# Forward stage: places of the group two back ahead of the normalisation, its gates behind it, both ahead of the second gate product

## The chip, the core and the metric

The kernel runs on one core of a Trainium2 chip. Its engines are TensorE (PE in the rows, its weight loads PEld), VectorE (DVE), ScalarE (ACT), GpSimd (POOL) and SyncE (SP, which only issues transfers here). Each has its own stream of instructions and waits for the others by semaphores. The metric is the time of one execution on the device in microseconds (us); lower is better.

## The reference, cut to what matters

Two layers of attention-like and feed-forward blocks over 8 x 512 tokens of 128 features. The change lies where the third block ends (its adapted weights `theta` applied to the queries) and the fourth, a mixture of eight experts, chooses its rows.

```python
    h_q = jax.nn.swish(q_ttt @ theta['gate']) * (q_ttt @ theta['val'])
    o = h_q @ theta['proj'] @ proj_w + proj_b
...
    logits = xt @ Wg + bg
    probs = jax.nn.softmax(logits, axis=-1)
    gate_vals, exp_idx = jax.lax.top_k(probs, K)          # K = 2 of E = 8
    gate_vals = gate_vals / jnp.sum(gate_vals, axis=-1, keepdims=True)
    capacity = int(np.ceil(CF * T * K / E))
    eidx = exp_idx.T.reshape(-1)
    oh = jax.nn.one_hot(eidx, E, dtype=jnp.int32)
    pos = jnp.sum((jnp.cumsum(oh, axis=0) - oh) * oh, axis=-1)
    keep = pos < capacity
    buf = buf.at[eidx, pos_c].add(jnp.where(keep[:, None], xk, 0.0))
```

`xt` is the layer-normalised sum of the input and `o`. So for each token the kernel needs its normalisation, its two experts, the two gates, and its place in each expert's list, which is a count over the tokens before it.

## The kernel before, in words

The forward stage works in eight groups (`g`) of 512 tokens, four tiles of 128. The hidden width of 512 is worked in four chunks (`c`), numbered through as `z = 4g + c`. What each engine does in a group, in its written order (nothing is scheduled by a program; the order in the code is the order on the engine):

- TensorE: for each chunk two products of 128 x 512 (gate and value, into a ring of three pairs of banks); behind chunk 0, from g = 2, `earlier_choices(g - 2)`, the small counting matmuls (64, then up to 48 columns) whose sum is `pos`; they wait for the choices of that group and for the router sums of group g - 1. Behind chunk 3 comes `fwd_out(g)`, the output product: 16 matmuls (32 rows of the trace) of 136 columns into four quarters of two banks. It waits for all four gate products of VectorE. A product of TensorE for chunk c = 3 waits for the gate product of chunk 0 of its group, one of the next group's chunk 0 for that of chunk 1.
- ScalarE: silu of each chunk (L1446); ahead of chunk 2 `scaled_tokens(g - 1)` (L1432, four instructions), which waits for the normalisation.
- VectorE: `moments(g - 1)` (L2296 the residual add, which waits for the output product, L2299 the router sums, mean and variance up to L2314); then the gate products of the four chunks (L2421, here called products 0 to 3), each of which waits for its silu; behind product 0 `normalise_tokens(g - 1)` (L2320 to L2330), which waits for GpSimd's power; behind product 1, from g = 2, `gates_of(g - 2)` (L2376 to L2380) and `places(g - 2)` (L2390 to L2402); behind product 3 `choices(g - 1)` (L2342 to L2369).
- GpSimd: a power L1130 (the root of the variance of group g - 1 and the exponential of group g - 2 in one instruction), which waits for the moments; then the last two scatters of the group before (L1116, indirect transfers that write rows of tokens to the experts' lists in HBM), and then six scatters of group g - 2, which wait for that group's gates, scaled tokens and places.

Behind the eight groups two more rounds (g = 8 and 9) finish the choices, in the order places, normalisation, gates at g = 8. When all 64 scatters have landed, the experts' rows are loaded.

The steps inside normalisation, gates and places each wait for the one ahead on the same engine. All three parts write tiles that the others don't read.

Of the kernel before, what the change touches and what calls it, by code (L numbers as in the profile page):

```python
# [33 lines left out]
def build(nc, L0_attn_x, L0_attn_W_pe, L0_attn_b_pe, L0_attn_stt_energy, L0_attn_W_fc, L0_attn_gamma,  # L34
# [18 lines left out]
    with ExitStack() as ctx:  # L53
# [115 lines left out]
        CHUNKS = [(24, 7), (18, 6), (12, 6)]  # L169
        NCH = len(CHUNKS)  # L170
        CH_END = [sum(n for _, n in CHUNKS[:c + 1]) for c in range(NCH)]
        v_taps = [(k, c) for c, (lo, n) in enumerate(CHUNKS) for k in range(lo + n - 1, lo - 1, -1)]
        assert len(v_taps) == NDVE and NPOOL % PT == 0
# [1794 lines left out]
        def _(dve):  # L1968
# [87 lines left out]
            for b in range(NB):  # L2056
                more, i = b + 1 < NB, 0
                for what in DVE_ORDER:
                    kind, g = what.rstrip("0123"), int(what[-1]) if what[-1] in "0123" else 0
# [231 lines left out]
            def moments(g):  # L2291

                base = RS * g
                dve.wait_ge(f_o.sem, f_o.at(g + 1))
                tiles = slice(g * TPB, (g + 1) * TPB)
                TT(X[:, tiles, :], quarter[:, :, 0:D], X[:, tiles, :], ALU.add).then_inc(x3_ready.sem, x3_ready.unit)  # L2296
                if g == 0:
                    dve.wait_ge(rt["lx"].sem, rt["lx"].at(3))
                TT(GL, quarter[:, :, D:D + NE], router_x[:, tiles, :], ALU.add).then_inc(rt["raw"].sem, rt["raw"].unit)  # L2299
                dve.wait_ge(x3_ready.sem, x3_ready.at(g + 1))  # L2300
                for j in range(TPB):
                    ins = v.bn_stats(g_stats[:, j, :], X[:, g * TPB + j, :])
                ins.then_inc(rs.sem, rs.unit)
                dve.wait_ge(rs.sem, rs.at(base + 1))
                mean_e, m2_e, mean_o, m2_o = (g_stats[:, :, f] for f in (1, 2, 4, 5))
                TT(gs[:, 0, :], mean_e, mean_o, ALU.add)
                TT(gs[:, 1, :], mean_e, mean_o, ALU.subtract)
                TT(gs[:, 2, :], m2_e, m2_o, ALU.add).then_inc(rs.sem, rs.unit)
                dve.wait_ge(rs.sem, rs.at(base + 2))
                v.tensor_scalar(gs[:, 8, :], gs[:, 0, :], 0.5, None, ALU.mult)  # L2310
                v.tensor_scalar(gs[:, 5, :], gs[:, 2, :], 1.0 / D, LN_EPS, ALU.mult, ALU.add)
                v.scalar_tensor_tensor(gs[:, 6, :], gs[:, 1, :], 0.25, gs[:, 1, :], ALU.mult, ALU.mult).then_inc(rs.sem, rs.unit)
                dve.wait_ge(rs.sem, rs.at(base + 3))
                TT(powers[:, 0, 0:TPB], gs[:, 5, :], gs[:, 6, :], ALU.add).then_inc(rt["ve"].sem, rt["ve"].unit)  # L2314

            def normalise_tokens(g):

                base = RS * g
                dve.wait_ge(rt["inv"].sem, rt["inv"].at(g + 1))
                TT(gs[:, 5, :], powers[:, 2, 0:TPB], powers[:, 2, 0:TPB], ALU.mult).then_inc(rs.sem, rs.unit)  # L2320
                dve.wait_ge(rs.sem, rs.at(base + 4))
                TT(gs[:, 6, :], gs[:, 5, :], powers[:, 0, 0:TPB], ALU.mult).then_inc(rs.sem, rs.unit)
                dve.wait_ge(rs.sem, rs.at(base + 5))
                v.tensor_scalar(gs[:, 5, :], gs[:, 6, :], -0.5, 1.5, ALU.mult, ALU.add).then_inc(rs.sem, rs.unit)
                dve.wait_ge(rs.sem, rs.at(base + 6))
                if g:
                    dve.wait_ge(rt["xn"].sem, rt["xn"].at(g))
                TT(gs[:, 7, :], gs[:, 5, :], powers[:, 2, 0:TPB], ALU.mult).then_inc(rs.sem, rs.unit)
                dve.wait_ge(rs.sem, rs.at(base + 7))
                v.scalar_tensor_tensor(gs[:, 12, :], gs[:, 8, :], -1.0, gs[:, 7, :], ALU.mult, ALU.mult).then_inc(rt["scale"].sem, rt["scale"].unit)  # L2330
# [40 lines left out]
            def gates_of(g):  # L2371

                tiles, gt = slice(g * TPB, (g + 1) * TPB), rt["gated"]
                ratio, first, apart = powers[:, 2, TPB:], XR[:, tiles, D + 1], XR[:, tiles, D + 2]
                dve.wait_ge(rt["inv"].sem, rt["inv"].at(g + 2))
                v.tensor_scalar(gg, ratio, 1.0, None, ALU.add).then_inc(gt.sem, gt.unit)  # L2376
                dve.wait_ge(gt.sem, gt.at(3 * g + 1))
                v.reciprocal(first, gg).then_inc(gt.sem, gt.unit)
                dve.wait_ge(gt.sem, gt.at(3 * g + 2))
                v.scalar_tensor_tensor(apart, ratio, -1.0, first, ALU.add, ALU.mult).then_inc(gt.sem, gt.unit)  # L2380

            def places(g):

                tiles, ps, base = slice(g * TPB, (g + 1) * TPB), rt["place"], PS * g
                oh = OHK[:, tiles, :]
                dve.wait_ge(rt["prefix_mm"].sem, rt["prefix_mm"].at(g + 1))
                dve.wait_ge(rt["index"].sem, rt["index"].at(g + 1))
                at = D + NE
                pos = quarter[:, 3, at:at + TPB * NEK].rearrange("p (c e) -> p c e", e=NEK)
                v.tensor_scalar(gk[:, 0], pos, float(CAP), 1e6, ALU.is_ge, ALU.mult)  # L2390
                TT(gk[:, 1], pos, place_sign[:].unsqueeze(1).to_broadcast([P, TPB, NEK]), ALU.mult).then_inc(ps.sem, ps.unit)
                dve.wait_ge(ps.sem, ps.at(base + 1))
                TT(gk[:, 2], gk[:, 1], place_base[:].unsqueeze(1).to_broadcast([P, TPB, NEK]), ALU.add)
                TT(run[:], run[:], gr, ALU.add).then_inc(ps.sem, ps.unit)
                dve.wait_ge(ps.sem, ps.at(base + 2))
                TT(gk[:, 1], gk[:, 0], gk[:, 2], ALU.add).then_inc(ps.sem, ps.unit)
                dve.wait_ge(ps.sem, ps.at(base + 3))
                TT(gk[:, 3], gk[:, 1], oh, ALU.mult).then_inc(ps.sem, ps.unit)
                dve.wait_ge(ps.sem, ps.at(base + 4))
                v.tensor_reduce(gp.rearrange("p c k -> p (c k)"), gk[:, 3].rearrange("p c (k e) -> p (c k) e", e=NE), AX.X, ALU.add).then_inc(ps.sem, ps.unit)  # L2400
                dve.wait_ge(ps.sem, ps.at(base + 5))
                v.tensor_copy(put_at[:, g * TPB * TOPK:(g + 1) * TPB * TOPK], gp.rearrange("p c k -> p (c k)")).then_inc(rt["put"].sem, rt["put"].unit)  # L2402
                dve.wait_ge(rt["put"].sem, rt["put"].at(g + 1))

            dve.wait_ge(rt_made.sem, rt_made.at(10))
            for g in range(NB + 2):
                if 1 <= g <= NB:
                    moments(g - 1)
                if g < NB:
                    s = g % 2  # L2410
                    for c in range(HC):
                        z = g * HC + c
                        if c == 1 and g:
                            normalise_tokens(g - 1)
                        if c == 2 and g >= 2:
                            gates_of(g - 2)
                            places(g - 2)
                        dve.wait_ge(f_sr.sem, f_sr.at(z + 1))
                        if c == 0:
                            dve.wait_ge(f_o.sem, f_o.at(g + 1 - 2))  # L2420
                        TT(f_h[:, s, c, :], f_s[:, z % FRING, :], bank[2 * (z % FRING) + 1][:], ALU.mult).then_inc(f_hr.sem, f_hr.unit)  # L2421
                elif g == NB:
                    places(g - 2)
                    normalise_tokens(g - 1)
                    gates_of(g - 2)
                else:
                    places(g - 2)
                    gates_of(g - 2)
                if 1 <= g <= NB:
                    choices(g - 1)  # L2430
# [110 lines left out]
```

## Time and profile before

| | us |
|---|---|
| median of three runs | 1357.92 (1357.22 to 1360.12) |
| the profiled execution, its own time | 1356.87 |
| its span in the profile | 1354.8 |
| busy: TensorE / VectorE / GpSimd / ScalarE | 1131.4 / 902.9 / 542.5 / 489.7 |
| forward stage, first gate product to the last output product's add | 1008.2 to 1121.9 |
| tail of scatters behind it, last one starts | 1149.3 |

The shares are means over stages with different limits, so the prediction reads the forward stage alone. In a row of the timeline stand: start, duration, engine, line, operation, what it writes and reads, how many instructions are merged, and in brackets the idle time of the engine ahead of it and what ended that.

### The profile page before, as it was taken

How to read it: one execution, taken by the hardware profiler on the slowest of the kernel's cores; microseconds unless marked ns; L12 is line 12 of the kernel's file. 1: busy time of each engine (PE TensorE's matmuls, PEld its weight loads, DVE VectorE, ACT ScalarE, POOL GpSimd, SP SyncE). 2: the span in 40 equal slices, each digit the busy share in tenths (PEclk: the TensorE clock that was granted, in tenths of full speed). 3: DMA queues.
4: the chain of work that ended last, by engine and by line, in shares of the span. 5: the costliest groups of instructions: out<-in, count | busy, mean ns of one | idle time of the engine just before them, and what ended most of it. 6: DMA issues, size and time to landing. Idle time of an engine off the chain costs nothing.

```text
span 1354.8 us, 15992 instructions
## 1 busy us (share of the span) xinstructions
PE 1131.4 (84%) x4801; PEld 682.0 (50%) x4801; DVE 902.9 (67%) x2031; ACT 489.7 (36%) x957; POOL 542.5 (40%) x453
## 2 busy tenths in 40 slices
PE   3899999964867668999999899999989872798981
PEld 1444444432456454555556555555555541575761
DVE  5788888888889686777777577777746673423220
ACT  3544444445435563222223222222232220455441
POOL 4788788984346234000000000000003557176776
PEclk9899999986989988999999999999999896898996
DMA  4422222200000041000080000000000122556432
GB/s 138 123 60 60 61 60 60 60 0 1 0 1 0 6 158 63 16 23 15 23 324 20 1 24 15 23 15 16 17 8 28 52 87 94 138 115 132 75 42 22
DMA packets 66191, 73.86 MB, mean 55 GB/s; under 512 B 10223, under 2 KB 44369, under 8 KB 65617
## 3 DMA queue, kind: packets, MB, share of 16 engines
q1 hardware_dynamic: 52369, 64.46, 15.3%
q0 software_dynamic: 13504, 8.62, 4.4%
q8 instruction: 29, 0.48, 0.1%
q14 instruction: 33, 0.27, 0.1%
q10 hardware_dynamic: 256, 0.03, 0.0%
HBM read 29.73 MB, written 28.02 MB: 43 GB/s over the span
## 4 chain that ended last, share of the span: by engine, by line
PE 36%; POOL 9%; issue 9%; DVE 4%; DMA 2%; ACT 1%; POOLq 1%; SPq 0%; DVEq 0%; ACTq 0%
PE banks L1708 33%; POOL out_dram L1154 6%; POOL expert_in_scratch L1116 2%; PE banks L1743 2%; DMA out_dram<-arena 2%; POOL powers L1130 1%; PE banks L1763 1%; DVE arena L2421 0%; DMA arena<-expert_in_scratch 0%; ACT arena L1401 0%; DVE arena L2273 0%; DVE arena L2277 0%; DVE arena L2281 0%; DMA expert_in_scratch<-arena,put_at 0%; POOLq L53 0%
## 5 line engine op out<-in xcount | busy, mean ns | idle before, releaser
L1708 PE MATMUL banks<-arena 128*128 128x128 f32 (+4 forms) x1480 | 381.9, 396 | 16.3 <-ACT arena L1467 7.2
L1708 PEld LDWEIGHTS banks<-arena 128*128 128x128 f32 (+1 forms) x1480 | 204.3, 190 | 88.0 <-issue 57.5
L1580 PE MATMUL banks<-arena,ident 128*128 128x512 f32 x368 | 172.4, 600 | 10.8 <-DVE arena L2038 9.6
L1154 POOL DMA_INDIRECT out_dram<-arena x80 | 127.7, 1596 | 71.6 <-issue 35.6
L1022 POOL TENSOR_TENSOR arena<-arena 128x512 f32<-128x512 f32 x96 | 112.3, 1196 | 14.3 <-ACT arena L1195 14.3
L1580 PEld LDWEIGHTS banks<-arena,ident 128*128 128x128 f32 x368 | 67.0, 191 | 87.4 <-issue 64.0
L1112 POOL IOTA arena<- 128x32 f32 x1 | 0.2, 215 | 262.7 <-DVE ttt_val_w L2284 262.7
L1388 ACT ACTIVATE arena<-banks 128x512 f32<-128x512 f32 x64 | 38.2, 597 | 175.1 <-PE banks L1743 175.1
L2038 DVE TENSOR_TENSOR arena<-arena,banks 128x512 f32<-128x512 f32 x152 | 96.1, 674 | 0.5 <-PE banks L1580 0.5
L1708 PEld LDWEIGHTS banks<-ttt_proj_w,arena 128*128 128x128 f32 x512 | 67.8, 194 | 31.7 <-issue 29.2
L1029 POOL TENSOR_TENSOR arena<-arena 128x512 f32<-128x512 f32 x64 | 81.3, 1270 | 5.0
L1110 POOL TENSOR_TENSOR router_x<-router_x,router_b 128x256 f32<-128x256 f32 x1 | 0.7, 727 | 204.3 <-ACT router_b L1409 204.3
L2223 DVE TENSOR_TENSOR arena<-arena,banks 128x512 f32<-128x512 f32 x64 | 44.0, 687 | 51.3 <-PE banks L1708 51.1
L1116 POOL DMA_INDIRECT expert_in_scratch<-arena,put_at x64 | 62.9, 982 | 33.5 <-issue 21.8
L1708 PE MATMUL banks<-ttt_proj_w,arena 128*128 128x128 f32 x512 | 68.6, 278 | 0.0
L1708 PE MATMUL banks<-ttt_gate_w,arena 128*128 128x512 f32 x128 | 67.2, 607 | 0.7 <-issue 0.7
L1708 PE MATMUL banks<-ttt_proj_wT,arena 128*128 128x512 f32 x128 | 65.6, 594 | 0.7 <-ACT arena L1393 0.7
L1708 PE MATMUL banks<-ttt_val_w,arena 128*128 128x512 f32 x128 | 66.0, 598 | 0.0
L1382 ACT ACTIVATE arena<-banks 128x512 f32<-128x512 f32 x64 | 38.2, 598 | 69.6 <-PE banks L1708 68.4
L2209 DVE TENSOR_TENSOR arena<-banks,arena 128x512 f32<-128x512 f32 x64 | 44.2, 691 | 15.2 <-PE banks L1708 15.2
L1467 ACT ACTIVATE arena<-banks,b_s 128x410 f32<-128x410 f32 (+1 forms) x84 | 49.2, 600 | 10.1 <-PE banks L1708 5.0
L1454 ACT ACTIVATE arena<-arena 128x128 f32<-128x128 f32 x80 | 26.0, 391 | 72.4 <-DVE arena L2478 62.1
(351 smaller groups left out, 2123.0 us busy)
## 6 DMA issues: line engine op xcount, KB each, us to landing
arena<-arena SPq DMA_DIRECT2D x64, 224.0 KB
arena<-expert_in_scratch SPq DMA_DIRECT2D x14, 589.5 KB
expert_in_scratch<-arena SPq DMA_DIRECT2D x4, 1244.5 KB
expert_in_scratch<-arena SPq DMA_DIRECT2D x5, 982.5 KB
arena<-kT_scratch SPq DMA_DIRECT2D x16, 256.0 KB, 2.6
arena<-k_scratch SPq DMA_DIRECT2D x16, 256.0 KB, 2.6
arena<-in_L_ffn_W_dram SPq DMA_DIRECT2D x16, 256.0 KB
kT_scratch<-arena SPq DMA_DIRECT2D x8, 256.0 KB
```

Source lines behind the costliest of these rows:

```text
L1022: pool.tensor_tensor(out=by_heads(dst), in0=window(b, k), in1=ws[:, b % 2, :, k:k + 1].to_broadcast([P, HT, HD]), op=ALU.mult).then_inc(po ...
L1029: ins = pool.tensor_tensor(out=unit, in0=unit, in1=ptmp[:, i, :], op=ALU.add)
L1116: pool.indirect_dma_start(out=buf_dram, out_offset=bass.IndirectOffsetOnAxis(ap=put_at[:, a:a + 1], axis=0), in_=XR[:, a // TOPK, :], in_o ...
L1154: pool.indirect_dma_start(out=out_rows_dram, out_offset=bass.IndirectOffsetOnAxis(ap=y_at[0:r, s, j:j + 1], axis=0), in_=yo[0:r, q, j % 4, ...
L1382: nc.scalar.activation(t_sig[:, q, :], bank[0][:], ACT.Sigmoid).then_inc(tt["sig"].sem, tt["sig"].unit)
L1388: nc.scalar.activation(hT[:, q, :], bank[2][:], ACT.Copy).then_inc(tt["hT"].sem, tt["hT"].unit)
L1467: nc.scalar.activation(hE[:, c, at:at + w], bank[2 + q][:, 0:w], ACT.Gelu_apprx_tanh, bias=b1_s[:, s, c:c + 1]).then_inc(ex["gelu"].sem, e ...
L1580: m = nc.tensor.matmul(bank[ACC[b % 2]][:], ident[:], src, start=first, stop=last)
L1708: return nc.tensor.matmul(out_, lhsT, rhs, start=start, stop=stop)
L2038: nc.vector.tensor_tensor(by_heads(prodv[:, n % NV, :]), window(b, k), bank[WB[q % 2]][:, (k - lo) * HT:(k - lo + 1) * HT].unsqueeze(2).to ...
L2209: TT(t_da[:, q, :], bank[4][:], t_m[:, q, :], ALU.mult).then_inc(tt["da"].sem, tt["da"].unit)
L2223: TT(t_h[:, q, :], t_s[:, q, :], bank[1][:], ALU.mult).then_inc(tt["h"].sem, tt["h"].unit)
```

## The change

In groups 2 to 7, VectorE does the places of the group two back directly behind product 0, ahead of the normalisation, and that group's gates directly behind the normalisation, ahead of product 1. Before, both stood between products 1 and 2. Products 1, 2 and 3 then follow one another. The rounds g = 0, 1, 8 and 9 and all other engines keep their order. A line is added, so the gate product's line is L2422 in the changed kernel.

```diff
@@ -2410,11 +2410,12 @@
                     s = g % 2
                     for c in range(HC):
                         z = g * HC + c
+                        if c == 1 and g >= 2:
+                            places(g - 2)
                         if c == 1 and g:
                             normalise_tokens(g - 1)
-                        if c == 2 and g >= 2:
+                        if c == 1 and g >= 2:
                             gates_of(g - 2)
-                            places(g - 2)
                         dve.wait_ge(f_sr.sem, f_sr.at(z + 1))
```

VectorE in group 2 before, from the last instruction of the moments to the start of places; semaphores are shared by names, so ln_std stands for the power and wqT_mm for the counting matmuls:

```order
L2314 TENSOR_TENSOR powers<-arena 128x4 [waits fp4_step]
L2421 TENSOR_TENSOR arena<-arena,banks 128x512 [waits f_o,f_s]
L2320 TENSOR_TENSOR arena<-powers 128x4 [waits ln_std]
L2322 TENSOR_TENSOR arena<-arena,powers 128x4 [waits fp4_step]
L2324 TENSOR_SCALAR arena<-arena 128x4 [waits fp4_step]
L2328 TENSOR_TENSOR arena<-arena,powers 128x4 [waits ln_out,fp4_step]
L2330 SCALAR_TENSOR_TENSOR arena<-arena 128x4 [waits fp4_step]
L2421 TENSOR_TENSOR arena<-arena,banks 128x512 [waits f_s]
L2376 TENSOR_SCALAR arena<-powers 128x4 [waits ln_std]
L2378 RECIPROCAL arena<-arena 128x4 [waits e_exp]
L2380 SCALAR_TENSOR_TENSOR arena<-powers,arena 128x4 [waits e_exp]
L2390 TENSOR_SCALAR arena<-banks 128x64 [waits wq_ready,wqT_mm]
```

The same engine from the same place in the changed kernel, up to the instruction that waits for the power:

```order
L2314 TENSOR_TENSOR powers<-arena 128x4 [waits fp4_step]
L2422 TENSOR_TENSOR arena<-arena,banks 128x512 [waits f_o,f_s]
L2390 TENSOR_SCALAR arena<-banks 128x64 [waits wq_ready,wqT_mm]
L2391 TENSOR_TENSOR arena<-banks,place_sign 128x64
L2393 TENSOR_TENSOR arena<-arena,place_base 128x64 [waits nrm_step]
L2394 TENSOR_TENSOR run<-run,arena 128x16
L2396 TENSOR_TENSOR arena<-arena 128x64 [waits nrm_step]
L2398 TENSOR_TENSOR arena<-arena 128x64 [waits nrm_step]
L2400 TENSOR_REDUCE arena<-arena 128x8 [waits nrm_step]
L2402 CAST put_at<-arena 128x8 [waits nrm_step]
L2320 TENSOR_TENSOR arena<-powers 128x4 [waits ln_std,q_scaled]
```

So the wait for the counting matmuls has moved ahead of the wait for the power. Further on in the same group of the changed kernel, from the end of the normalisation to the start of the choices:

```order
L2330 SCALAR_TENSOR_TENSOR arena<-arena 128x4 [waits fp4_step]
L2376 TENSOR_SCALAR arena<-powers 128x4 [waits ln_std]
L2378 RECIPROCAL arena<-arena 128x4 [waits e_exp]
L2380 SCALAR_TENSOR_TENSOR arena<-powers,arena 128x4 [waits e_exp]
L2422 TENSOR_TENSOR arena<-arena,banks 128x512 [waits f_s] x3
L2342 TENSOR_TENSOR arena<-arena 128x32 [waits unit_ready,xqT_mm]
```

Before, product 1 stood ahead of L2376, and places stood between L2380 and the other two products.

## Rows read from the trace of the kernel before

**Rows 1.** Waits of DVE, 1005 to 1180 us: waiter, releaser, us, times, longest

```profile
DVE X L2296 <- PE banks L1708: 14.2, 6, 4.1
```

**Rows 2.** Timeline of one group on DVE: residual add to products 2 and 3

```profile
1060.24 0.69 DVE L2296 TENSOR_TENSOR X<-banks,X 128x512 f32<-128x512 f32 x1 [3.53 <-PE banks L1708]
...
1062.64 0.69 DVE L2421 TENSOR_TENSOR arena<-arena,banks 128x512 f32<-128x512 f32 x1
...
1064.51 0.16 DVE L2320 TENSOR_TENSOR arena<-powers 128x4 f32<-128x4 f32 x1 [1.19 <-POOL powers L1130]
...
1064.90 0.17 DVE L2324 TENSOR_SCALAR arena<-arena 128x4 f32<-128x4 f32 x1
...
1065.38 0.68 DVE L2421 TENSOR_TENSOR arena<-arena,banks 128x512 f32<-128x512 f32 x1
...
1065.98 0.23 DVE L2376 TENSOR_SCALAR arena<-powers 128x4 f32<-128x4 f32 x1
...
1066.54 0.22 DVE L2390 TENSOR_SCALAR arena<-banks 128x64 f32<-128x64 f32 x1
...
1068.25 1.28 DVE L2421 TENSOR_TENSOR arena<-arena,banks 128x512 f32<-128x512 f32 x2
```

**Rows 3.** Timeline of the same group on PE and ACT

```profile
1061.60 0.79 PE L1708 MATMUL banks<-arena,ident 128*128 128x48 f32 x6
...
1065.50 1.65 ACT L1432 ACTIVATE arena<-X,arena 128x128 f32<-128x128 f32 x4 [0.66 <-DVE arena L2330]
...
1067.05 1.22 ACT L1446 ACTIVATE arena<-banks 128x512 f32<-128x512 f32 x2
...
1069.59 3.98 PE L1708 MATMUL banks<-PW,arena 128*128 128x136 f32 x32 [1.95 <-DVE arena L2421]
```

**Rows 4.** Timeline of the same group on POOL: power, second late scatter, first of six

```profile
1062.81 1.67 POOL L1130 TENSOR_TENSOR powers<-powers 128x8 f32<-128x8 f32 x1 [2.38 <-DVE powers L2314]
...
1066.01 0.97 POOL L1116 DMA_INDIRECT expert_in_scratch<-arena,put_at  x1 [0.30 <-issue]
...
1069.10 0.97 POOL L1116 DMA_INDIRECT expert_in_scratch<-arena,put_at  x1 [2.12 <-DVE put_at L2402]
```

**Rows 5.** Timeline: output products and the adds behind them, three groups

```profile
1026.22 3.97 PE L1708 MATMUL banks<-PW,arena 128*128 128x136 f32 x32 [1.41 <-DVE arena L2421]
...
1030.23 0.69 DVE L2296 TENSOR_TENSOR X<-banks,X 128x512 f32<-128x512 f32 x1 [0.91 <-PE banks L1708]
...
1076.27 0.69 DVE L2296 TENSOR_TENSOR X<-banks,X 128x512 f32<-128x512 f32 x1 [3.52 <-remote]
...
1116.66 3.97 PE L1708 MATMUL banks<-PW,arena 128*128 128x136 f32 x32 [1.95 <-DVE arena L2421]
...
1121.92 0.69 DVE L2296 TENSOR_TENSOR X<-banks,X 128x512 f32<-128x512 f32 x1 [2.10 <-PE banks L1708]
```

**Rows 6.** Timeline of the end of the stage, rounds g = 8 and 9

```profile
1123.28 0.79 PE L1708 MATMUL banks<-arena,ident 128*128 128x48 f32 x6
...
1124.49 1.67 POOL L1130 TENSOR_TENSOR powers<-powers 128x8 f32<-128x8 f32 x1 [0.94 <-issue]
...
1124.89 0.23 DVE L2390 TENSOR_SCALAR arena<-banks 128x64 f32<-128x64 f32 x1 [0.49 <-PE banks L1708]
...
1125.28 0.22 DVE L2393 TENSOR_TENSOR arena<-arena,place_base 128x64 f32<-128x64 f32 x1
...
1126.60 0.16 DVE L2320 TENSOR_TENSOR arena<-powers 128x4 f32<-128x4 f32 x1
...
1126.99 0.37 DVE L2324 TENSOR_SCALAR arena<-arena 128x4 f32<-128x4 f32 x1
...
1149.29 0.97 POOL L1116 DMA_INDIRECT expert_in_scratch<-arena,put_at  x1 [0.30 <-issue]
```

**Rows 7.** Windows (busy of PE, PEld, DVE, ACT, POOL, then PEclk) and timeline: a slower output product

```profile
1055.50:1057.50 2.00, 2.00 (x11) 2.00 (x10) 1.08 (x6) 0.00 (x0) 1.57 (x2) 0.52 0.20 67
...
1053.56 5.64 PE L1708 MATMUL banks<-PW,arena 128*128 128x136 f32 x32 [1.99 <-DVE arena L2421]
```

## The prediction

> **What bounds the kernel now.** I read the views in this order: the waits of VectorE over the forward stage, one group on all engines in order of time, and last the end of the stage. No engine is at its limit there: TensorE, ScalarE, VectorE and GpSimd hand each group on to each other. The largest wait of VectorE within the stage is the one of the residual add L2296 for the output product, 14.2 in six waits [rows 1]. I look at the group that begins when that add starts at 1060.24 [rows 2] and ends when it starts again at 1076.27 [rows 5]: 16.03 us.
>
> In it one cycle runs: add at 1060.24, moments, product 0 at 1062.64 [rows 2]; GpSimd's power from 1062.81, 1.67 long [rows 4]; VectorE idles 1.19 and starts the normalisation at 1064.51 [rows 2]; product 1 at 1065.38, gates at 1065.98, places at 1066.54, products 2 and 3 from 1068.25, ending 1069.53 [rows 2]; the output product of TensorE at 1069.59 [rows 3]; the next add at 1076.27 [rows 5]. So 9.35 us belong to the add-to-output-product part and 6.68 to the output product until VectorE sees it.
>
> The second part is longer than the matmuls. Without scatters running, the output product started at 1026.22 and the add followed at 1030.23, 4.01 later. Here it is 6.68, and in the last group 1121.92 - 1116.66 = 5.26 [rows 5]. The excess, 1.25 to 2.67 in these two, is there only in groups in which GpSimd scatters. GpSimd itself isn't the bound before the last group: it idles before each run of six scatters (2.12) [rows 4] and before the power. After the last moments it is: from 1124.49 it works without a pause worth naming to the last scatter at 1149.29 [rows 6], and the experts' first load waits for that. What the change brings must therefore bring 1124.49 forward.
>
> **The change part by part.** No instruction is added or removed. In groups 2 to 7 the eight instructions of places go ahead of the normalisation, into the idle time behind product 0; the three of gates go ahead of product 1.
>
> Places, 1068.25 - 1066.54 = 1.71 [rows 2]. Now it can start one product pitch (1065.98 - 1065.38 = 0.60) behind product 0: 1063.24. Its input, the counting matmuls, begin their last part at 1061.60 and take 0.79 [rows 3], so it doesn't wait. It ends at 1064.95. The power is ready for VectorE at 1064.51: of the 1.71, 1.27 lie in idle time and 0.44 delay the normalisation. The cover is thus the 1.19 of idle time [rows 2] and some wake-up time; without it places would cost its whole 1.71.
>
> Normalisation, 1065.38 - 1064.51 = 0.87, from 1064.95: ends 1065.82. Gates, 0.56, to 1066.38. Products 1, 2 and 3 at a pitch of 0.60 could then start at 1066.38, 1066.98 and 1067.58 on VectorE, against 1068.85 for product 3 before. This 1.27 is not what comes out, for ScalarE is next: it scales the tokens when the normalisation is ready (1065.50, that is 0.99 after its start), runs the third activation 1.55 later at 1067.05, and two activations take 1.22 [rows 3]. With the normalisation 0.44 later: 1065.94, 1067.49, 1068.71. Product 3 follows at 1068.74, takes 0.68, and the output product starts at about 1069.48 instead of 1069.59. **Gain 0.11.**
>
> One thing takes this back. At the end of the stage (g = 8, already ordered places, normalisation) the tensor_scalar L2324 took 0.37 [rows 6], where it takes 0.17 in the group [rows 2]. It started 0.83 behind the end of the power (1126.99 against 1126.16), with a scatter under way. In the changed groups it starts at 1064.95 + 0.39 = 1065.34, 0.86 behind the end of the power, at the same phase of the same scatter. I count 0.20 more: output product at 1069.68, **0.09 later than before**. Both ends stay: -0.11 and +0.09; I take the second, as the row is nearest in kind.
>
> This holds for the four groups in which TensorE idles about 1.95 before the output product, as in [rows 3, 7]. In the timeline of TensorE the other two idle 1.41, as the group without places does [rows 5]: there the last activation already sets product 3, and 0.44 to 0.64 of delay fit into its slack: nothing. Sum: 4 x 0.09 = +0.4, bounds -0.4 and +0.4.
>
> The scatters move too. Places' result comes at 1064.95 instead of 1068.25, gates' at 1066.38 to 1066.58. GpSimd is still in its two late scatters: the second starts at 1066.01, lasts 0.97 [rows 4], so 1066.98, and about 0.44 behind it the run of six begins: 1067.42 instead of 1069.10, **1.7 earlier**. At a pitch of 1.28 its last scatter then begins at 1073.8 and ends at 1074.8, before 1076.5. By itself that gains nothing, as GpSimd waits for the next moments anyway, and after the last moments the tail of scatters is as long as before. It changes only what lies beside the output product.
>
> Product 1 comes up to 1.2 us later. Nobody misses it: of its readers the earliest is the next group's first pair of matmuls, behind the output product. The earlier end of places frees the output product's bank earlier, and that wait isn't the last one either.
>
> **Clock.** One output product ran at the granted clock 0.52, that is the 1.2 GHz level, after TensorE had idled 1.99, and took 5.64 instead of 3.97 [rows 7]. The idle times before and after stay within 0.2 of what they were, so I count no change, but 1.7 us per such product for the range.
>
> **The rivals.** *A, the likeliest:* only the order's sum. The profiled run took 1356.87 (its span 1354.8 and 2.1 around it); with +0.4 it is 1357.3. The median of the runs is 1.05 above the profiled one, so 1358.3. With the bounds of the sum and one output product at the other clock level more or less: 1356.0 to 1360.4.
>
> *B, the output product's end is seen earlier.* For it: the delay beyond 4.01 exists only in groups with scatters, and the six now end sooner. Before, the add started 0.8 behind the start of the sixth scatter (1069.10 + 5 x 1.28 = 1075.5, and 1076.27) [rows 4, 5]. If that bounds it, the add now comes by 1073.8 + 0.8 = 1074.6, a gain of 1.6 in this group. The last group, whose delay is 1.25, would gain about 0.4 by the same rule, and the four between some 2 in all: 4 us, hence 1354.3; if the delay went altogether, 1351. Against it: the six scatters still cover the whole output product, and under the same six scatters one group shows an excess of 2.67 and the last 1.25. This trace doesn't show what makes it.
>
> *C, slower: places waits for the counting matmuls.* Places now stands ahead of everything that ScalarE and the output product wait for. At the end of the stage the counting matmuls ended at 1123.28 + 0.79 = 1124.07, and places, with VectorE idle, started only at 1124.89, 2.97 behind the add [rows 6]. In a changed group its turn comes 3.00 behind the add (1063.24 - 1060.24): a slack of 0.03. Each us that the matmuls are seen later is then a us for the group. With 0.6 in each of six groups: 1358.3 + 3.6 = 1361.9. It decides from 0.5 per group. Against it: the matmuls ended 0.9 before that turn in this group, and the late arrival at the end of the stage still lies before this point.
>
> *D, GpSimd's power and places hold each other out.* Places now runs under the power, and L2393, L2396 and L2398 read two operands in SBUF. If they waited for its end, L2393 would move from 1063.63 to 1064.5: 0.9 more in up to six groups, 1363. The end of the stage speaks against it: the power ran from 1124.49 to 1126.16, L2393 started at 1125.28, and places took 1126.60 - 1124.89 = 1.71 [rows 6], as long as without a power beside it.
> By the Trainium skill ("SBUF — State Buffer", Who interferes with whom) such an instruction and a GpSimd instruction that reads SBUF exclude each other for the whole instruction, which is the time of D; the trace doesn't agree for these small shapes.
>
> That the change does not do what it says is excluded for the order itself, but not for its purpose: if product 3 is set by ScalarE, nearly nothing of the freed time arrives. That is A.
>
> **How the numbers follow.** A 0.53, B 0.27, C 0.16, D 0.04. A difference of 0.2%, 2.7 us, is about what measurement can tell from none. B lies beyond it on one side, C and D on the other, A within; so faster 0.27, same 0.53, slower 0.20. The range 1353.4 to 1361.5 takes in A whole and reaches into B and C until 2 in 10 are out.
>
> **What would show it.** Right: in a changed group the idle time before the normalisation is gone, places takes 1.71 about 0.6 behind product 0, the run of six scatters starts about 4.8 behind product 0 instead of 6.5, and the output product about 7.0 behind it as before. L2324 at 0.37 shows the loss, at 0.17 the gain. B would show as less than the 5.3 to 6.7 between the output product and the add; C as idle time before L2390, released by TensorE; D as a stretched L2393. Wrong would be a product 3 that is not released by ScalarE, or a different count of output products at the lower clock.

## The result and the profile after

| | before | changed |
|---|---|---|
| median of 20 runs each, us | 1357.78 (1355.07 to 1361.22) | 1362.15 (1358.02 to 1364.06) |
| profiled execution, its own time / its span | 1356.87 / 1354.8 | 1362.42 / 1360.4 |
| first residual add of the stage / last one | 1017.98 / 1121.92 | 1019.27 / 1127.32 |
| between these two | 103.94 | 108.05 |
| last add to the end of the last scatter | 28.34 | 28.17 |

The ratio of the runs is 1.0023, with a 95% interval of 1.0013 to 1.0032. So the changed kernel is slower by 3.1 us (0.0023 x 1357.8; by the interval 1.8 to 4.3), which gives 1360.9 where 1358.3 was predicted. The medians are 4.4 apart. In the two profiles the stage is 4.1 longer. Another 1.3 lies ahead of the first changed instruction and isn't the change's. Each profile shows one execution, and the 20 times of either kernel spread over 6 us: the two profiled times are 5.6 apart, the runs 3.1 to 4.4. So the group-by-group figures below belong to these two executions.

First the group that begins at 1047.24, on VectorE, as [rows 2] of before (start, duration, engine, line, operation; in brackets the idle time ahead and its releaser):

```profile
1047.24 0.69 DVE L2296 TENSOR_TENSOR X<-banks,X 128x512 f32<-128x512 f32 x1 [3.26 <-remote]
...
1049.64 0.69 DVE L2422 TENSOR_TENSOR arena<-arena,banks 128x512 f32<-128x512 f32 x1
1050.24 0.22 DVE L2390 TENSOR_SCALAR arena<-banks 128x64 f32<-128x64 f32 x1
...
1050.62 0.23 DVE L2393 TENSOR_TENSOR arena<-arena,place_base 128x64 f32<-128x64 f32 x1
...
1051.95 0.16 DVE L2320 TENSOR_TENSOR arena<-powers 128x4 f32<-128x4 f32 x1
...
1052.34 0.35 DVE L2324 TENSOR_SCALAR arena<-arena 128x4 f32<-128x4 f32 x1
...
1053.55 0.68 DVE L2422 TENSOR_TENSOR arena<-arena,banks 128x512 f32<-128x512 f32 x1
1055.28 1.28 DVE L2422 TENSOR_TENSOR arena<-arena,banks 128x512 f32<-128x512 f32 x2 [1.05 <-ACT arena L1446]
...
1063.26 0.69 DVE L2296 TENSOR_TENSOR X<-banks,X 128x512 f32<-128x512 f32 x1 [3.53 <-remote]
```

The order does what it was worked out to do. Places begin 0.60 behind product 0 (1050.24) and take 1.71 to 1051.95; there is no idle time ahead of L2390 nor of L2320; L2324 takes 0.35. Product 2 starts when ScalarE has released it. Product 3 then follows on VectorE at the pitch of 0.60: the two activations of ScalarE are over at 1055.73 (below, 1054.68 + 1.05), ahead of its start at 1055.89. The same group on TensorE:

```profile
1056.62 3.97 PE L1708 MATMUL banks<-PW,arena 128*128 128x136 f32 x32 [1.99 <-DVE arena L2422]
1060.43 1.02 PE L1708 MATMUL banks<-arena,ttt_gate_w 128*128 128x512 f32 x2
1061.29 1.02 PE L1708 MATMUL banks<-arena,ttt_val_w 128*128 128x512 f32 x2
...
1073.75 3.97 PE L1708 MATMUL banks<-PW,arena 128*128 128x136 f32 x32 [1.41 <-DVE arena L2422]
```

and on ScalarE:

```profile
1053.12 1.65 ACT L1432 ACTIVATE arena<-X,arena 128x128 f32<-128x128 f32 x4 [1.29 <-DVE arena L2330]
1054.68 1.05 ACT L1446 ACTIVATE arena<-banks 128x512 f32<-128x512 f32 x2
1063.31 0.60 ACT L1446 ACTIVATE arena<-banks 128x512 f32<-128x512 f32 x1 [7.58 <-PE banks L1708]
```

The output product starts 6.98 behind product 0 (1056.62 - 1049.64), against 6.95 before. That is the whole of the order's own effect: 0.03 later. Groups 4 and 7 of the changed kernel are another case, told under the clock further down: there the output product starts 8.1 behind product 0.

GpSimd, the same group: the power, the first late scatter, the first of six and the last:

```profile
1049.81 1.67 POOL L1130 TENSOR_TENSOR powers<-powers 128x8 f32<-128x8 f32 x1 [3.62 <-DVE powers L2314]
1051.67 1.04 POOL L1116 DMA_INDIRECT expert_in_scratch<-arena,put_at  x1 [0.20 <-issue]
...
1054.43 0.97 POOL L1116 DMA_INDIRECT expert_in_scratch<-arena,put_at  x1 [0.45 <-issue]
...
1060.82 0.97 POOL L1116 DMA_INDIRECT expert_in_scratch<-arena,put_at  x1 [0.30 <-issue]
```

The six begin 4.79 behind product 0 instead of 6.46, as predicted. What came out otherwise is the last piece, from the start of the output product to the next add. Group by group (2 to 7), in us, read off the timelines of both (the time from product 0 to the output product is the difference of two rows):

| group | 2 | 3 | 4 | 5 | 6 | 7 |
|---|---|---|---|---|---|---|
| before: output product to add | 4.59 | 6.68 | 6.68 | 5.92 | 5.30 | 5.26 |
| changed: output product to add | 6.36 | 6.63 | 5.51 | 6.70 | 6.61 | 5.49 |
| before: product 0 to add | 11.55 | 13.66 | 13.63 | 14.00 | 12.24 | 12.21 |
| changed: product 0 to add | 13.32 | 13.61 | 13.61 | 13.68 | 13.59 | 13.58 |
| before: period, add to add | 13.95 | 16.06 | 16.03 | 16.40 | 14.65 | 14.61 |
| changed: period | 15.72 | 16.02 | 16.01 | 16.08 | 15.98 | 15.99 |

Groups 3 to 5 are as long as before or 0.4 shorter together. All of the loss is in groups 2, 6 and 7: 1.77 + 1.33 + 1.38 = 4.5, less 0.4 makes the 4.1. By pieces, the time from the output product to the add grew by 2.9 in sum (34.4 to 37.3), and the time from product 0 to the output product by 1.2 (two groups with 8.1 instead of one). Before, three groups got their add earlier than 13 behind product 0; in the changed kernel none does.

The add isn't waiting for the matmuls as the profile shows them, whose ends are modelled. The output product of 1056.62 and the pair behind it end at 1060.59 and 1062.31 (1061.29 + 1.02), 1.72 apart. Yet the add that needs the first starts at 1063.26 and the silu that needs the second at 1063.31, 0.05 apart. And in the next group, product 0 at 1065.65, the output product starts 1.12 later in the group (1073.75) and its add comes at the same place all the same, 13.61 behind product 0:

```profile
1079.26 0.69 DVE L2296 TENSOR_TENSOR X<-banks,X 128x512 f32<-128x512 f32 x1 [2.38 <-remote]
```

The waits of VectorE, 1005 to 1180 us (waiter, releaser, us, times, longest). In the kernel before, two more waits of the add stand beside the 14.2 in six of [rows 1], so 20.5 in eight:

```profile
DVE X L2296 <- remote: 6.3, 2, 3.5
```

In the changed kernel they are 23.7 in eight:

```profile
DVE arena L2422 <- ACT arena L1446: 15.8, 10, 6.3
DVE X L2296 <- remote: 12.7, 4, 3.5
DVE X L2296 <- PE banks L1708: 11.0, 4, 4.1
```

"remote" means that the view finds no matmul whose end lies close enough ahead of the release. The release itself is on record: in both traces the semaphore of the output product is updated 0.02 ahead of each of the eight adds. In group 1 that is 0.01 behind the recorded end of the last matmul, in the groups with scatters 0.6 to 2.7 behind it. So VectorE starts at once; what is late is the update. The trace can't tell whether TensorE finished late or told it late. The updates of the scatters' semaphore, however, are missing in numbers here: of 1024 (16 for each of 64 scatters) the trace of before holds 501, that of the changed kernel 475.

### The profile page after: what moved, and what is told of

Same layout as the page of the kernel before. It is cut to its first block, busy times and chain, and to the rows that moved or that the text cites. A ratio compares the mean times of both kernels' runs of the same rounds, so it can differ in the third digit from the quotient of the medians.

```text
span 1360.4 us, 15992 instructions
## 1 busy us (share of the span) xinstructions
PE 1135.7 (83%) x4801; PEld 684.4 (50%) x4801; DVE 904.5 (66%) x2031; ACT 489.7 (36%) x957; POOL 541.2 (40%) x453
## 4 chain that ended last, share of the span: by engine, by line
PE 39%; issue 8%; POOL 5%; DVE 4%; DMA 2%; ACT 2%; another core or an unknown queue 0%; POOLq 0%; SPq 0%; DVEq 0%; ACTq 0%
PE banks L1708 37%; POOL out_dram L1154 5%; PE banks L1743 2%; DMA out_dram<-arena 2%; DVE arena L2422 1%; PE banks L1763 1%; DMA arena<-expert_in_scratch 0%; ACT arena L1432 0%; ACT arena L1401 0%; ACT arena L1446 0%; DVE arena L2273 0%; DVE arena L2302 0%; DVE X L2296 0%; DVE arena L2277 0%
## 5 line engine op out<-in xcount | busy, mean ns | idle before, releaser
L1708 PE MATMUL banks<-arena 128*128 128x128 f32 (+4 forms) x1480 | 384.3, 398 | 15.8 <-ACT arena L1467 6.8
L1116 POOL DMA_INDIRECT expert_in_scratch<-arena,put_at x64 | 62.8, 981 | 22.1 <-issue 19.2
L2479 DVE TENSOR_TENSOR arena<-banks,b_b 128x512 f32<-128x512 f32 x16 | 11.1, 692 | 61.5 <-PE banks L1708 44.9
```

The lines of the kernel that those rows point to most:

```text
L1116: pool.indirect_dma_start(out=buf_dram, out_offset=bass.IndirectOffsetOnAxis(ap=put_at[:, a:a + 1], axis=0), in_=XR[:, a // TOPK, :], in_o ...
L1708: return nc.tensor.matmul(out_, lhsT, rhs, start=start, stop=stop)
```

## Experiments

Behind all runs stand two ways to explain the result. By the first, scatters that run beside the output product hold back its release, by how they lie against it; the change put them elsewhere, and pays for that. By the second, the release is late for a reason that has nothing to do with where the scatters lie, and the change is worth its own sum, or what it does to GpSimd's queue. Runs sent together share a chip, and so do their runs of the kernel before; the chips turned out to differ, so every ratio below is against the kernel before on its own chip.

### One part alone, and the scatters put back

Places alone (gates stay where they were):

```diff
+                        if c == 1 and g >= 2:
+                            places(g - 2)
                         if c == 1 and g:
                             normalise_tokens(g - 1)
                         if c == 2 and g >= 2:
                             gates_of(g - 2)
-                            places(g - 2)
```

> Of the change only one half: places ahead of the normalisation, gates where they stood, behind product 1. GpSimd's six scatters wait for the later of the two, so they should start about 5.9 us behind product 0 (gates end there), against 6.46 before and 4.8 in the changed kernel, and no longer directly behind the two late scatters. Theory S (an unbroken run of eight scatters delays the moment at which VectorE sees the output product's end): output product to add between the before and the changed kernel, time 0 to 2 us above before. Theory O (the order on VectorE itself costs, wherever the scatters are): as the changed kernel, 3 to 4 us above before.

Gates alone (places stay):

```diff
-                        if c == 2 and g >= 2:
+                        if c == 1 and g >= 2:
                             gates_of(g - 2)
+                        if c == 2 and g >= 2:
                             places(g - 2)
```

> The other half alone: gates directly behind the normalisation, places where they stood, behind product 1. The six scatters wait for places and so keep their start, about 6.5 us behind product 0. Theory S: no cycle longer than before, time within 1 us of before. Theory O: some part of the 3 to 4 us, the more the more gates ahead of product 1 matters.

The changed kernel with its six scatters held until product 2 of the group:

```diff
                     pool.wait_ge(rt["put"].sem, rt["put"].at(g - 1))
+                    if g < NB:
+                        pool.wait_ge(f_hr.sem, f_hr.at(g * HC + 3))
```

> The changed kernel whole, with one wait added on GpSimd: in groups 2 to 7 the run of six scatters also waits until product 2 is written, so it starts about 7.2 us behind product 0 instead of 4.8. VectorE's order is that of the changed kernel. Theory S: the time between output product and add returns to what it was before (4.6 to 6.7) or less, cycles of 14.6 to 16.0, time within 1 us of before. Theory O: the time stays 3 to 4 us above before.

The changed kernel with all 64 scatters behind the last round:

```diff
-                    for a in range((g - 2) * GA - LATE, (g - 2) * GA):
-                        scatter(a)
...
-                    for a in range((g - 2) * GA, (g - 1) * GA - LATE):
-                        scatter(a)
-            for a in range(NA - LATE, NA):
+            for a in range(NA):
                 scatter(a)
```

> The changed kernel with no scatter in the forward stage: all 64 are issued behind the last round, so the tail of scatters is longer by some 48 x 1.28 = 61 us and the whole time is not the question. Read is the forward stage alone: if scatters are what delays the sight of the output product's end, the add follows 4.0 us behind its start in every group and a cycle takes 13.4 us; if the order on VectorE does it, the 6.6 us and the 16.0 us stay.

Measured: the kernel before has 1348.38 on this chip, not 1357.8. Places alone 1345.9, ratio 0.9983 (0.9974 to 0.9992). Gates alone 1348.66, 1.0005 (0.9995 to 1.0014). The hold 1348.71, 1.0008 (0.9999 to 1.0017). Without scatters in the stage 1412.15, one run: they then all stand behind it.

The main surprise is common to all four: the output product is seen 4.01 behind its start in every group but one (5.68 in one group of the hold, at the 1.2 GHz level of TensorE's clock), whether scatters run beside it or not. The late release that takes up to 2.7 us a group in the recorded runs is not there. So scatters beside the output product aren't enough to make it, and e4 could not tell the two explanations apart here. And places alone gains, which by the prediction's sum should bring nothing. The hold shows why, on GpSimd: last scatter of the six, power, first of the next six (the two added lines move the gate product to L2424 and the normalisation to L2322):

```profile
1089.62 0.97 POOL L1116 DMA_INDIRECT expert_in_scratch<-arena,put_at  x1 [0.30 <-issue]
1090.60 1.68 POOL L1130 TENSOR_TENSOR powers<-powers 128x8 f32<-128x8 f32 x1
...
1097.12 0.96 POOL L1116 DMA_INDIRECT expert_in_scratch<-arena,put_at  x1 [2.33 <-DVE arena L2424]
```

The power has no idle time ahead of it: it starts when the last scatter ends, 1.16 behind product 0 (1089.44) instead of 0.17. VectorE pays for it ahead of the normalisation:

```profile
1092.39 0.16 DVE L2322 TENSOR_TENSOR arena<-powers 128x4 f32<-128x4 f32 x1 [0.67 <-POOL powers L1130]
```

The period is 13.87 in such groups, 13.39 with places alone.

### The changed kernel and the one before on a further chip

Both without an edit.

> The changed kernel once more, beside the kernel before, since in the four runs so far the add followed the output product 4.0 us behind its start in all groups but one, even with scatters beside it, while both traces on record show up to 6.7. Theory E (the excess behind the output product belongs to the conditions of a run, and only where it is there does the earlier run of scatters cost): if the excess is absent, the changed kernel's cycle is 13.4 us, as in e1_places, and its time 1 to 3 us below before; if it is there, 16.0 us and 3 to 4 us above. Theory O (order on VectorE): 3 to 4 us above before in either case.

> The kernel before, for its trace beside the changed one's. Theory E without excess: output product to add 4.0 us everywhere; the cycle is then set by GpSimd, whose six scatters start 6.5 us behind product 0 and end 13.8 behind it, later than the next power is wanted (13.6), so 13.6 to 13.9 us, against 13.4 in the changed kernel. With excess: 14 to 16 us as on record.

Changed: 1346.79, ratio 0.9981 (0.9972 to 0.9990), so 0.2% **faster** here, clear of noise. Before: median 1349.19. The kernel before, waits of VectorE:

```profile
DVE arena L2320 <- POOL powers L1130: 10.2, 8, 1.8
DVE X L2296 <- PE banks L1708: 10.1, 8, 4.1
```

its GpSimd (last of six, power, first of the next six):

```profile
1063.09 0.97 POOL L1116 DMA_INDIRECT expert_in_scratch<-arena,put_at  x1 [0.30 <-issue]
1064.08 1.69 POOL L1130 TENSOR_TENSOR powers<-powers 128x8 f32<-128x8 f32 x1
...
1070.39 0.98 POOL L1116 DMA_INDIRECT expert_in_scratch<-arena,put_at  x1 [2.12 <-DVE put_at L2402]
```

and its VectorE (add, product 0, normalisation, next add):

```profile
1061.19 0.69 DVE L2296 TENSOR_TENSOR X<-banks,X 128x512 f32<-128x512 f32 x1 [0.84 <-PE banks L1708]
...
1063.59 0.69 DVE L2421 TENSOR_TENSOR arena<-arena,banks 128x512 f32<-128x512 f32 x1
1065.80 0.16 DVE L2320 TENSOR_TENSOR arena<-powers 128x4 f32<-128x4 f32 x1 [1.53 <-POOL powers L1130]
...
1074.89 0.69 DVE L2296 TENSOR_TENSOR X<-banks,X 128x512 f32<-128x512 f32 x1 [0.84 <-PE banks L1708]
```

The period is 13.70. In it GpSimd has no pause before the power, though it still waits 2.12 for places. So a circle through GpSimd and VectorE **is** the bound there: power, normalisation, product 1, gates, places, six scatters, power. It costs some 0.32 (the power starts 0.49 behind product 0 instead of 0.17). In the changed kernel on the same chip, GpSimd:

```profile
1060.94 1.67 POOL L1130 TENSOR_TENSOR powers<-powers 128x8 f32<-128x8 f32 x1 [1.42 <-DVE powers L2314]
...
1065.56 0.97 POOL L1116 DMA_INDIRECT expert_in_scratch<-arena,put_at  x1 [0.44 <-issue]
...
1071.94 0.97 POOL L1116 DMA_INDIRECT expert_in_scratch<-arena,put_at  x1 [0.30 <-issue]
1074.33 1.67 POOL L1130 TENSOR_TENSOR powers<-powers 128x8 f32<-128x8 f32 x1 [1.41 <-DVE powers L2314]
```

The six end 1.4 before the power is wanted, which starts with the moments again. The period is 13.39; the stage from first to last add is 92.56 against 94.37, **1.8 shorter**, and the times 2.4 shorter. Of the 1024 updates of the scatters' semaphore the traces of this chip and the first hold 1015 or more.

### The three again side by side

The changed kernel, places alone and the one without scatters in the stage, as above.

> The changed kernel again, beside places alone and the kernel without scatters, to meet the excess behind the output product on one chip with all three. Without excess in the trace: cycles of 13.4 us and 1 to 3 us below before, as in f1_changed. With excess: cycles of 16.0 us and 3 to 4 us above before, as on record. A mixture (excess but faster, or none but slower) would speak against theory E.

> Places alone ahead of the normalisation; six scatters from 5.55 us behind product 0. Without excess as e1_places: cycles of 13.4 us, 1 to 3 us below before. With excess: if the unbroken run of eight scatters is what makes it worse (theory S), less than the changed kernel's 16.0 us a cycle, since 0.9 us of pause stand in the run; if not, 16.0 us as well.

> The changed kernel with all scatters behind the last round. If the other runs of this call show the excess, this one tells whether scatters in the stage are its cause: 4.0 us from output product to add in every group if they are, 5.5 to 6.7 if not. Without excess in the others: 13.37 us a cycle, nothing new.

Against 1348.92 for the kernel before: changed 1345.62, 0.9987 (0.9977 to 0.9997); places alone 1344.81, 0.9974 (0.9963 to 0.9986); without scatters 1413.15, nothing new. Both have a period of 13.39, so where the release isn't late the gates' move adds nothing to that of the places. The two intervals overlap: places alone isn't shown to be faster than the changed kernel.

### More transfers beside the stage

Can load on the transfers bring the late release back? Sixteen small writes of 16 rows x 512 bytes for each group, issued by SyncE to a scratch in HBM, behind the load of that group's queries, which runs ahead of the group; all results stay as they are. In the changed kernel the last of them is issued at 1097.93, so groups 6 and 7 have none beside their output product.

```diff
                 sp.dma_start(qT_l[:, s, :], qT_dram[bass.ds(g, 1)].rearrange("g p t -> (g p) t")).then_inc(q_load[s].sem, q_load[s].unit)
+                for j in range(KN):
+                    sp.dma_start(noise_dram[bass.ds(g * KN + j, 1)].rearrange("g p t -> (g p) t"), ident[0:16, :]).then_inc(noise_out.sem, noise_out.unit)
```

On the changed kernel:

> The changed kernel with 16 small transfers more in each group of the forward stage (16 rows of 512 bytes from SBUF to a scratch in HBM, issued by SyncE, nobody waits for them before the experts), so 256 more semaphore updates a group beside the scatters' 128. In the two traces on record about half of the scatters' semaphore updates are missing (501 and 475 of 1024), in the runs since then none. Theory R (the excess is the sight of TensorE's semaphores held up where more updates come than the path that carries or records them takes): updates go missing here too, the add follows the output product later than 4.0 us, and cycles are longer than 13.4 us. Theory N (it has nothing to do with their number, but with the chip or what runs beside it): 4.0 us and 13.4 us as without the transfers, all updates in the trace.

On the kernel before:

> The kernel before with the same 16 transfers in each group. Theory R: an excess here as well, and against h1_noise the sign of the record, that is the changed order is the slower one by 1 to 4 us. Theory N: cycles of 13.7 us as in f2_before, and the changed order faster by 1 to 3 us.

On the changed kernel with the hold of e3 as well:

> The changed kernel with the sixteen small transfers per group of the run h1_noise, and also with the six scatters held until product 2 (as in e3_hold). It tells different things on the two kinds of chip seen so far. On a chip where the add follows the output product 4.01 behind its start (as chips 3 and 5): if extra transfers by themselves make the late release of the add, it becomes 5 to 6.7 in groups 3 to 7, the period 15 to 16 and the time 10 to 14 above e3_hold's 1348.7; if they do not, 4.01 stays, the period stays 13.4 to 13.9 and the time within 3 of 1348.7. On a chip with the late release (as the recorded runs and chip 11): if what matters is the unbroken run of eight scatters from 2.0 to 12.1 behind product 0, the hold puts a pause of some 2.6 into it and the period falls from 16.0 towards the 14.6 of the faster groups before, up to 8 less than h1_noise's 1361.45 or a ratio to before of 0.997 to 1.000; if what matters is that scatters run under the output product at all, the hold moves more of them there, the add comes at 13.6 or later behind product 0 and the ratio is 1.003 or more.

These went to two chips on which the kernel before, without the transfers, takes about as long as in the recorded runs: 1356.26 on that of the first two and 1357.85 on that of the third. No run without the transfers was profiled there. With the transfers, changed: 1361.45, ratio 1.0027 (1.0009 to 1.0046), with the times and periods of the recorded run (15.8 to 16.1). Before: 1373.05, 1.0119 (1.0084 to 1.0154), periods 16.2 to 19.2. Changed with the hold: 1376.0, 1.0122 (1.0101 to 1.0143), periods 15.4 to 19.9. From the output product to the add it has 6.44, 6.73, 5.60, 6.76, 6.64 and 5.54 in groups 2 to 7, each within 0.1 of the recorded changed kernel's, so in that order the transfers add next to nothing. The waits of VectorE for the residual add (the added lines move it to L2302 and L2304), in the changed kernel with transfers:

```profile
DVE X L2302 <- remote: 15.4, 5, 3.6
DVE X L2302 <- PE banks L1714: 8.6, 3, 4.1
```

in the kernel before with transfers:

```profile
DVE X L2302 <- remote: 25.7, 6, 5.1
```

and in the changed one with transfers and hold:

```profile
DVE X L2304 <- remote: 23.5, 5, 5.8
```

In that last one the output product of the group that begins at 1051.94:

```profile
1062.41 3.97 PE L1716 MATMUL banks<-PW,arena 128*128 128x136 f32 x32 [1.41 <-DVE arena L2430]
```

and its add, 8.14 later:

```profile
1070.55 0.69 DVE L2304 TENSOR_TENSOR X<-banks,X 128x512 f32<-128x512 f32 x1 [4.97 <-remote]
```

Group 1, which has no scatters, settles one thing. In the changed kernel with transfers SyncE issues 16 of them from 1025.19 on (their rows on SyncE, then output product and add):

```profile
1025.19 8.04 SPq L885 DMA_DIRECT2D noise_scratch<-ident  x16
...
1025.86 3.97 PE L1714 MATMUL banks<-PW,arena 128*128 128x136 f32 x32 [1.41 <-DVE arena L2428]
...
1029.87 0.69 DVE L2302 TENSOR_TENSOR X<-banks,X 128x512 f32<-128x512 f32 x1 [0.91 <-PE banks L1714]
```

The add comes 4.01 behind the output product, as without them. So on the very chip that shows the late release, these transfers without scatters don't make it; and group 6, with scatters and none of these transfers, has 6.64.

What follows. On these chips the place of the six scatters does count, as the hold shows, which leaves VectorE's order alone: with the transfers there, from 4.79 behind product 0 the add comes at 13.4 to 13.7; from 6.5 and later (before) at 13.8 to 16.8; held to 7.2 and later at 15.9 to 17.5 in five groups and 13.0 in the last. The hold alone costs 14.6 us between two runs that are otherwise the same (1376.0 against 1361.45; on two chips whose kernels before are 1.6 apart). Not all of it is the release: with the hold the output product itself starts 8.07 to 9.77 behind product 0 in four groups; from it to the add it is 8.92, 8.14, 8.03, 7.81, 6.24 and 6.04. That the harm is in eight scatters running without a break, one form of the first explanation, falls with it: the hold put a break into the run and made it worse. The opposite form, that scatters further under the output product do more harm, fits these three runs, but not the recorded pair, in which the earlier scatters went with the later add. Whether extra transfers would bring the late release to a chip that doesn't have it wasn't seen: all three runs fell on chips that are as slow as the recorded one anyway. The hold and places alone without extra transfers weren't run on such a chip.

## Why the prediction was off

The number first. 1360.9 lies within the range of 1353.4 to 1361.5, the median of 1362.15 beyond it. The forecast was A, nothing that measurement can tell; measured is a small loss, with the wait for the output product changed, which A held fixed. That the time came out within 2.6 to 3.9 us of 1358.3 is luck: where the release isn't late, the same change is 1.8 to 2.6 us faster (0.9987 and 0.9981).

**The order's sum** held. Places hidden under the power, 0.44 of delay for the normalisation, ScalarE's chain as the limit, L2324 at its longer duration: all are in the rows of after, and the output product came 0.03 later in its group where 0.09 was summed; over four groups that is 0.1 and not 0.4, within the bounds. One link was wrong: ScalarE releases product 2, and product 3 only follows it at VectorE's pitch, since the two activations took 1.05 instead of 1.22. By the prediction's own words ("a product 3 that is not released by ScalarE") that was a sign of being wrong; it cost nothing. The bounds that it gave A, 1356.0 to 1360.4, are up to 0.4 too high for its own terms: 1357.92 less and plus 0.4 and 1.7 makes 1355.8 to 1360.0.

**The step that failed** is the one that the rest hung on: that the time from the output product to the add stays what it was in each group. The profile before had it at 4.59 to 6.68 with no pattern that I could name, and I took it over as a constant of the group. It was no such thing: in groups 2, 6 and 7 it went from 4.59, 5.30 and 5.26 to 6.36, 6.61 and 5.49, and over the six groups it grew by 2.9. That is most of the 4.1 us by which the stage is longer, against +0.4 predicted; the other 1.2 stand ahead of the output product (see the clock below). What made it grow stays open.

**B** (the add released by the end of the scatters) had the sign wrong on record. The six scatters do end 1.7 earlier, and the add didn't follow. With 13.6 behind product 0 in five groups the add stands 1.5 behind the end of the last scatter (1060.82 + 0.97 = 1061.79 to 1063.26), where it stood ahead of it before. The objection written down against B, that one group showed an excess of 2.67 and another 1.25 under the same scatters, was the right one; it spoke against A's constant just as well, and there I didn't use it.

**"By itself that gains nothing"**, on the earlier scatters, failed in another way: it is true only as long as the late release leaves GpSimd its pause. Where the add comes 4.01 behind the output product, GpSimd ends its six scatters after the power is wanted, and the 1.7 is worth 0.3 in each group. Two chips show the gain; gates alone (no gain) and the hold (the gain undone) show that it comes from the scatters' earlier start. I had written which engine isn't the bound from a profile in which a longer wait hid it.

**C** did not occur: L2390 follows product 0 at 0.60 in all six groups. The place of 1361.9 was near the measured time, for a reason that had no part in it.

**D** did not occur: L2393 ran from 1050.62 to 1050.85 under the power (1049.81 to 1051.48) in 0.23, and in the kernel before on the further chip, with no power beside it, in 0.22. By the Trainium skill ("SBUF — State Buffer", Who interferes with whom) a VectorE instruction with two inputs in SBUF contends with a GpSimd instruction that reads SBUF; at these shapes the trace shows nothing of it beyond the 0.01.

**Clock.** The prediction counted no change; the profile after has three stretches of the stage at the 1.2 GHz level instead of two. One of them comes shortly behind 1.83 of idle time of TensorE: from 1065.30 to 1068.40 the granted clock is 0.56. It and the third moved two output products to 8.10 behind product 0, where before it was one. In a sum of terms these are 1.2 us of the 4.1. But their adds came at 13.6 like the others, whose output products stood at 6.98, so it is likely, though not shown, that they cost nothing.

**What stays open** is what makes the late release. Known of it: it goes with the chip, or with something that stays the same on a chip over these runs (none on two chips at 1348.4 to 1349.2 for the kernel before, present in every profile from two at 1356.3 and 1357.9, all of them with the extra transfers, and in the recorded runs at 1357.8); it is seen only in groups with scatters, as group 1 without any has 4.01 in all traces; small transfers without scatters don't make it (group 1 with them); with them beside the scatters it grows in the order before and hardly in the changed order, and it grows with a later start of the six scatters then; it holds two releases of TensorE back to one moment; and it comes together with missing records of the scatters' semaphore updates (440 to 524 of 1024), while the late releases themselves are all on record. The scatters' own packets aren't slower where it occurs: their median is 0.19 us in the recorded pair and in the pair of the further chip. That records and releases are held up by the same thing would fit, but no run shows it.

## What to carry to other kernels

When a wait in the profile is longer than the work it waits for, and by different amounts in like groups, it is not a constant to be kept in the sum: look at how many groups are short, and price the case that none is any more. And an engine that has pauses only because another wait is long is not off the path: take that wait away in thought (here 16.0 to 13.4 us a group) and see which engine is then late, since this is what another chip will run. Moving work into idle time that is released by a third engine gained nothing by itself; what gained, where anything did, was the start of the transfers behind it.

## What the hardware showed unasked

- The same program takes 1348.4 and 1349.2 on two chips and 1356.3 and 1357.9 on two others, with the clock granted as a mean of 0.94 on all, and a change that is 0.1 to 0.2% faster on the first kind is 0.2% slower in the recorded runs.
- The release of the output product was updated up to 2.7 us behind the recorded end of its matmuls (up to 4.9 with transfers and hold), and the release of the matmuls behind it 0.05 later, where the matmuls' ends were 1.72 apart. In groups without scatters it was 0.01 behind.
- The tensor_scalar of 128 x 4 takes 0.35 instead of 0.17 when it starts 0.86 behind the end of the power, as the scatter behind it runs; it did so in the changed kernel on both kinds of chip. In group 2, where no scatter follows the power, it took 0.17 at 0.91 behind the power's end.
